# A four-layer kernel on one core: the attention heads of four engines written out in place of a loop

## The reference, cut to what matters

```python
q = einsum('btd,ndh->btnh', x, q_kernel)       # 16 query heads of 128
kv = einsum('bsd,ckdh->cbskh', x, kv_kernel)   # 8 key/value heads
q, k = rope(rms_norm(q, q_scale)), rope(rms_norm(k, k_scale))
mask = (j <= i) & (i - j < 256)
probs = softmax(where(mask, q @ k * ATTN_SCALE, min))
out = einsum('btnh,nhd->btd', probs @ v, out_kernel)
```

## Time and profile before

| | |
|---|---|
| median of 3 runs | 2092.71 us |
| lowest and highest of them | 2083.91 and 2093.48 us |
| the profiled execution, its own time | 2091.68 us |
| its span, first to last instruction | 2089.9 us |
| mean granted TensorE clock over the span | 0.978 |
| busy share of the span: PE, DVE, ACT, POOL | 94%, 72%, 57%, 37% |
| HBM read and written | 207.81 and 45.61 MB |

### The profile page before, as it was taken

The page is one execution under the profiler, slowest core; times in us unless marked ns, Lnnn a source line. Parts: engine busy times, 40 slices in busy tenths (PEclk is TensorE's granted clock), DMA queues, the critical chain, the costliest instruction groups (busy, mean ns, idle before and its releaser), DMA issues. The chain is left out here.

```text
span 2089.9 us, 33169 instructions
## 1 busy us (share of the span) xinstructions
PE 1974.8 (94%) x10142; PEld 1672.2 (80%) x10142; DVE 1504.8 (72%) x3538; ACT 1200.7 (57%) x2978; POOL 766.3 (37%) x1072
## 2 busy tenths in 40 slices
PE   7999999989999999999999989969989999999996
PEld 6677777768888888888888878757878898888875
DVE  7788555897776777677777768985467877775665
ACT  6752222576666666666666656764366776674342
POOL 3441000575555555555555546840600000000552
PEclk9999999999999999999999989989999999999998
DMA  7343010235000000000000000122789999984563
GB/s 259 126 139 128 26 36 21 91 126 162 21 12 21 10 21 10 21 11 1 21 10 21 30 1 16 52 76 96 250 313 326 314 316 311 314 313 144 200 206 117
DMA packets 82657, 245.03 MB, mean 117 GB/s; under 512 B 10800, under 2 KB 11440, under 8 KB 80592
## 3 DMA queue, kind: packets, MB, share of 16 engines
q1 hardware_dynamic: 77376, 226.46, 31.7%
q0 software_dynamic: 5120, 16.78, 2.2%
HBM read 207.81 MB, written 45.61 MB: 121 GB/s over the span
## 5 line engine op out<-in xcount | busy, mean ns | idle before, releaser
L282 PE MATMUL l_xp<-att_w_hi,xT_hi 128*128 128x512 f32 x512 | 210.2, 410 | 5.0 <-ACT att_qkv L2453 5.0
L282 PE MATMUL l_xp<-att_w_lo,xT_hi 128*128 128x512 f32 x512 | 203.5, 397 | 0.0
L282 PE MATMUL l_xp<-att_w_hi,xT_lo 128*128 128x512 f32 x512 | 203.4, 397 | 0.0
L921 POOL TENSOR_SCALAR att_pr<-att_pr,rec_ri 128x384 f32<-128x384 f32 (+2 forms) x256 | 141.3, 564 | 140.3 <-DVE rec_ri L1589 140.2
L2482 ACT ACTIVATE att_pr<-att_pr,rec_nb,rec_r 128x384 f32<-128x384 f32 (+2 forms) x256 | 168.5, 662 | 40.3 <-DVE rec_nb L1560 40.0
L1556 DVE CUSTOM_DVE_ANT_0 att_pr<-l_dd,att_mask 128x384 f32<-128x384 f32 (+2 forms) x256 | 119.5, 502 | 79.6 <-PE l_dd L282 62.7
L925 POOL TENSOR_TENSOR att_rot<-att_rot,att_rot 128x384 f32<-128x384 f32 x128 | 129.8, 1014 | 117.4 <-DVE att_rot L1583 117.4
L3913 POOL DMA_INDIRECT y<-moe_rows,moe_slotA x16 | 16.3, 1018 | 416.0 <-DMA moe_rows<-moe_lo_f 412.9
L2453 ACT ACTIVATE att_qkv<-l_xp 128x512 f32<-128x512 f32 x128 | 76.5, 598 | 145.6 <-PE l_xp L282 114.6
L1594 DVE TENSOR_TENSOR att_pT_lo<-l_out,att_pT_hi 128x768 fp32r<-128x768 f32 (+2 forms) x128 | 108.8, 850 | 24.8 <-ACT att_pT_hi L2475 24.5
L2475 ACT ACTIVATE att_pT_hi<-l_out 128x768 fp32r<-128x768 f32 (+2 forms) x128 | 92.5, 723 | 46.1 <-PE l_t L282 24.3
(11 more groups left out here) (327 smaller groups left out, 6563.5 us busy)
## 6 DMA issues: line engine op xcount, KB each, us to landing
y<-in_moe_rt SPq DMA_DIRECT2D x59, 704.0 KB, 6.1
y<-in_moe_rt SPq DMA_DIRECT2D x39, 768.0 KB, 6.5
moe_sraw_gu<-in_moe_sgu SPq DMA_DIRECT2D x44, 512.0 KB
moe_sraw_d<-in_moe_sd SPq DMA_DIRECT2D x44, 256.0 KB
moe_xs<-in_zeros SPq DMA_DIRECT2D x39, 256.0 KB, 7.1
moe_lo_f<-moe_xs SPq DMA_DIRECT2D x39, 256.0 KB, 6.8
moe_rows<-moe_lo_f SPq DMA_DIRECT2D x39, 256.0 KB, 6.4
att_raw_w<-in_qkv_w SPq DMA_DIRECT2D x8, 1024.0 KB, 4.8
```

The lines of the kernel that those rows point to most:

```text
L282: mm = pe.matmul(out, lhsT, rhs, start=(i == 0), stop=(i == len(terms) - 1))
L921: pool.tensor_scalar(p, p, ri[:, j % 2, g:g + 1], 1.0, ALU.mult, ALU.mult).then_inc(sa("p"), 1)
```

## The change

Each of the four loops on the engines becomes a loop of the Python program that writes the kernel: the six passes are written out one behind the other, with `k` a plain number, and every wait compares with a constant. The order of the steps on each engine stays as it was, head by head. SP's loop is left as it is.

```diff
@@ POOL @@
-            with pool.Fori(1, KVH - 1) as k:
+            for k in range(1, KVH - 1):
                 split_w_part(k, 1)
                 weigh(12, NT * k - 4)
...
@@ DVE @@
-            with dve.Fori(1, KVH - 1) as k:
+            for k in range(1, KVH - 1):
                 row_max(12, NT * k - 4)
                 split_w(k, 2)
...
@@ ACT @@
-            with act.Fori(1, KVH - 1) as k:
+            for k in range(1, KVH - 1):
                 split_w_part(k, 0)
                 squares(15, NT * k - 1)
...
@@ PE @@
-            with pe.Fori(1, KVH - 1) as k:
+            for k in range(1, KVH - 1):
                 turn_p(10, NT * k - 6)
                 project(k, 15, NT * k - 1)
```

## The result

| | before | after |
|---|---|---|
| median (4 runs each) | 2091.59 us | 2068.08 us |
| lowest and highest | 2083.91, 2093.48 us | 2064.03, 2070.00 us |
| profiled execution, its span | 2091.68, 2089.9 us | 2070.00, 2068.0 us |
| mean granted clock | 0.978 | 0.983 |
| packets of the two instruction queues | 57 and 104 | 83 and 83 |

The ratio is 0.9892, with a 95% interval of 0.9863 to 0.9921: faster by 23.5 us where 20.8 were forecast, and inside the range.

The account below looks back on a forecast made before the run. PE, busy 94% of the span, was taken to bound the kernel, waiting at five seams between loop passes. 2091.68 less 20.8 gave 2070.9 us, plus 1.0 for the median 2071.9; range 2062 to 2081 us.

Parts of the forecast that it names:

- the seam: Between two loop passes, five times: PE waits 3.0 us for DVE's `att_k_lo`; excess 4.2 us each, 20.8 in all.
- DVE's halts behind its branch: Before and in the middle of `row_max`: 2.73 and 1.52 us, delaying `split_qk`, whose last instruction PE waits for.
- ACT's halt: Behind ACT's own branch back, five times, 2.1 to 2.3 us; stands beside DVE's halts and goes too.
- The mark behind the last seam: Eviction of tile 0's projection after the fifth branch back, at 1120.46 us; used to price the five branches.
- the unstalled seam: First pass, entered without a jump: 14.12 us from tile 15's eviction to tile 0's, against 18.32 at the first branch back.
- The second sum of the prediction: Per branch back: PE's wait 3.0, less 0.5 that the first pass also has, plus 1.7 through the clock: 4.2 us.
- The register instructions: In the sequencers' streams between steps: counted at nothing, hidden by PE's work; if uncovered, 1.8 us a head.
- the code that must be brought: PE's body brought in all six written-out passes, 30 packets more: costed at nothing, as in the first pass.
- The clock: After PE's stand-still its clock is at 1.2 instead of 2.4 GHz for 3.3 us, costing up to 1.7 us.
- The margin: After the change DVE reaches `split_qk` 4.25 us earlier, PE waited 3.0, so DVE is 1.2 us ahead.
- A: Rival: only part of the loss between passes goes, 3.2 us each, 16 us in all; 2076.7 us; chance 0.13.
- B: Rival: each of 30 added code packets halts PE, 2.1 us each, 63 us before savings; 2135 us; chance 0.04.
- C: Rival: the halt between passes comes anyway, from new weights or step order; no change, 2092.7 us; chance 0.08.

Follow-up runs that it names:

- `u_pe_pool`: The kernel before with only PE's and POOL's loops written out, DVE and ACT left in their loops: 2090.98 us, ratio 1.0003 to the kernel before.
- `pairs`: The kernel before with all four engines' loops made three passes of two heads each: 2084.95 us, ratio 0.9972 to the kernel before.
- `u_dve`: The kernel before with only DVE's loop written out: 2078.05 us, ratio 0.9933 to the kernel before.
- `u_dve_act`: The kernel before with only DVE's and ACT's loops written out, PE and POOL left in theirs: 2068.03 us, ratio 0.9894 to the kernel before.

## Why the prediction was right

**The bound.** That the seam and not the body waits is shown: with the branches gone PE is busy 671.2 of 672.0 us in heads 1 to 6.

**The cause.** DVE's halts behind its branch, read off and the earlier trace rows, are shown as the cause from three sides: they go when DVE alone is written out, PE's wait stays when all but DVE and ACT are, and 4.0 us of useless work in their place brings the wait and the fallen clock back. Behind them stands ACT's halt, which the prediction only named as going too: with DVE's halts gone it is worth the other 10 us. That the halts are the bringing of code is read from the packets that fall into them and are absent in the changed kernel; the trace does not say for which engine a packet of that queue is.

**The size.** Forecast 20.8, measured 23.5 us between medians, and 21.7 between the profiled executions. The mark behind the last seam moved from 1120.46 to 1097.96 us, 22.5 us; since this execution came to head 1 1.9 us later (523.44 against 521.56), the heads themselves gave 24.4. The term that was undersized is the one that I took for the unstalled seam, 14.12 us. It was measured where head 0 ends, with a PE wait of 0.5 us for POOL, and I wrote that this wait stays in each head. It does not: later borders take 13.41 us, 5 x 0.7 = 3.5 us in all. The second sum of the prediction, 3.0 - 0.5 + 1.7 = 4.2 us a seam, agreed with the first only because it took off the same 0.5 us, once for each seam; the kernel before has that wait in head 1 alone, so nothing was to be taken off, and 3.0 + 1.7 = 4.7 is near the 4.9 us that a seam cost. That the two sums agreed was therefore no check.

**Parts costed at nothing.** The register instructions were right at nothing: head 1 took 112.79 us with them and 112.66 without, and `u_pe_pool` gains nothing. So was the code that must be brought: 26 packets more for PE, where 30 were counted, and no halt. The Trainium skill's sentence that crossing a border in straight code is mostly hidden ("Runtime: NRT & Kernel Launch", Instruction fetch mechanics) holds here. The prediction's count of ACT's body, some 220 rows, is too low: the trace has 396 records of ACT between two of its branches, with the steps on registers and semaphores and the reads of the accumulator. The body is longer than one block of 256 instructions, so its halts don't contradict the page that the prediction set them against.

**The clock.** I made the loss a sum of a 3.0 us wait and 1.7 us through the clock. The runs show both. By the marks, 1.6 us of wait costs 1.8 with the clock at 1.00, 2.6 costs 4.1 and 3.0 costs 4.9, each with 3.4 us or more at the lower level at its end or behind it.

**The margin.** 1.2 us was worked out, as 4.25 us of halts less 3.0 of waiting. It is half of that: with the halts gone DVE waits 0.5 us for PE's scores, so `att_k_lo` comes 3.8 us earlier and not 4.25, and it is written 0.63 us before PE needs it. This was luck in so far as nothing in the changed kernel uses up more.

**The rivals.** A (part stays) would have left an issue wait or a wait for `att_k_lo`: neither is there. B (straight code halts PE) did not come in any of the straight kernels. C (the seam waits anyway) is excluded by the borders of 13.41 us. That the price is the branch instruction's own, 0.5 us for all five by the Trainium skill's 108 ns ("Advanced Engine Details and Errata", Control Flow Timing), fails by a factor of some 45; the branches themselves took 40 ns on ACT to 238 ns on PE. What I did not see is that a loop can make PE halt too, as in `pairs`; the change does not meet it.

## What to carry to other kernels

Where engines run a loop each, look at the first instruction behind each branch back for an issue wait, and compare a pass with the first one, which had no jump ahead of it: the excess is the price, before anything is built. Write out the loop of the engine whose halt others wait for first, then the next: here two of four engines gave everything. Doubling a body to halve its branches can bring less than half of the gain (here 6 to 8 of some 23 us), when the body grows past what an engine keeps and a further engine begins to halt; and where straight code changes order, check that the new order starts as the old one ended.

## What the runs showed of the hardware that was not expected

- PE halts 2.9 us at a branch back when its body holds two heads, and does not halt (branch of 208 ns) when it holds one. DVE and ACT halt with a body of one head already, DVE 2.6 us at the first instruction of `row_max` and 1.6 us again at the second, ACT 2.1 us.
- PE waiting for DVE for 1.5 to 1.7 us left its granted clock at 1.00 at all five seams of `u_dve`; each of the waits for `att_k_lo` of 2.6 to 3.3 us at the seams of the other kernels came with a stretch at the lower level, 1.2 in place of 2.4 GHz, which began within 1.3 us of the wait's end. The length alone does not decide it: in `pairs` the clock fell behind PE's own halt of 3.05 us (0.83 from 742 to 752 us) and not behind that of 2.79 (1.00 from 976 to 985 us), and in `u_dve_act` and `pairs` it stayed at 1.00 behind a wait of 3.56 us for POOL before head 7.
- Written out, the code of the other engines came in fewer packets of its instruction queue than the loops took (31 against 50 in five heads), since the loops fetched parts of their bodies again in every pass and the register instructions are gone. With PE's 26 packets, which the loop did not need, the total rose from 50 to 57.
